# A two-layer recurrent and windowed-attention kernel: the second attention's key projection moves into free columns of the low-rank product

## The chip, the cores and the metric

The kernel runs on one core of one Trainium2 chip. The metric is the device time of one launch in microseconds (us), which covers all 16 sequences. In the text PE is TensorE, DVE is VectorE, ACT is ScalarE, POOL is GpSimd and SP is SyncE, whose queue issues every DMA transfer of this kernel.

## The reference, cut to what matters

Sixteen sequences of 1024 tokens with 256 features pass through two layers. Layer 0 is a gated recurrent attention with a mixture of experts as its gate. Layer 1, which the change touches, is attention in a window of 64 keys (16 query heads share 2 key/value heads of 16 features), gated by a two-matrix network with ternary weights and a low-rank term of rank 16.

```
def _L1_attn_ref(x, Wq, bq, Wk, bk, Wv, bv, Wo, bo):
    q = (x @ Wq + bq)...            # 16 heads of 16
    k = (x @ Wk + bk)...            # 2 heads of 16: 32 columns
    v = (x @ Wv + bv)...            # 2 heads of 16: 32 columns
    scores = jnp.einsum('bgrsd,bgswd->bgrsw', qg, k_win)   # window of 64 around each token
    probs = jax.nn.softmax(scores, axis=-1)
    ...
    return out @ Wo + bo

def _L1_ffn_ref(x, fast_b, w_fc, w_proj, u, v, gate):
    h = _bitlinear(x, w_fc) + gate * (x @ v.T @ fast_b.T @ u.T)
    r = jnp.maximum(h, 0.0)
    return _bitlinear(r * r, w_proj)

xn = _layernorm(x)
x = x + _L1_attn_ref(xn, ...) * _silu(_L1_ffn_ref(xn, ...))
```

## The kernel before, in words

One loop of two turns holds eight sequences written out one behind the other, so the body of a sequence runs 16 times. Each engine has its instructions in an order written out by hand; the engines meet only at semaphores. A sequence is cut into NC = 8 chunks of 128 tokens, and for wide products into NG = 2 groups of 512 tokens.

The stretch around the change is the seam between the layers. The layer-0 loop over the chunks `c` ends with `c = 7`. In it PE computes the recurrent outputs, turns (transposes) the normalised input of layer 1 into `xt`, two chunks at a time with `pair_turn`, and begins the projections of layer 1:

- `queries_keys(n)` for n = 0 to 5: three products of 512 columns for each group g = n // 3. Kinds 0 and 1 are the queries (`w_q2`, result `q2`, which lies in `qt`). Kind 2 is the keys: `w_k2r` holds the 32 key columns four times over, so the product puts the same 32 keys into all four groups of 32 rows. ACT evicts it twice (once for each key/value head, with `par_mask` as scale and `b_k2m` as bias, which zero the other head's rows) into `kt`, which lies in `k2`, shown as `k` in the rows.
- `low_rank(g)`: one product of 512 columns with `w_low`, whose 128 columns held the low-rank factor in columns 0, 32, 64 and 96 (16 each) and the two value heads in columns 16 to 31 and 48 to 63. ACT evicts it into `low_t`. Columns 80 to 95 and 112 to 127 were zero.
- `chunk_turn(6)` and `chunk_turn(7)`: the last two chunks of the layer-1 input are turned one at a time, since their normalisation comes late. ACT copies them out in `chunk_turned`.
- `output_turn(7)`, `output_turned(7)`, `output_project(7)`: the last output projection of layer 0 (PE, ACT into `yt`, PE).

After the seam comes the attention itself, a loop over the chunks: `score_masks(c)` puts the band mask into banks 1 to 4; `score_quad(c)` adds 32 small products of queries with keys, where group j of 32 rows works with `k2[32j:32j+32]`, so the keys must stand in all four row groups; DVE takes maxima and subtracts them (`maxima`, `shifted`); ACT takes the exponentials (`exps`); PE turns the probabilities (`probs_turn`, in two halves); ACT and DVE copy them out (`probs_turned`); PE multiplies by the values (`values`, `values_turn`). `window_values` turns the values out of `low_t`. `score_quad(3)` is the first that reads keys of the second group of 512 tokens.

The SP queue of one sequence holds the loads of `x`, the rows of the experts' gates, the loads of the next sequence's input behind the last `score_quad`, and the stores of the outputs. Before the loop SP also issues all weight and bias loads, one behind the other; PE's first product waits for all of them.

Of the kernel before, what the change touches and what calls it, by code (L numbers as in the profile page):

```python
# [48 lines left out]
def build_program(nc, a, out, n_seq):  # L49
# [107 lines left out]
    w_k2r = sb("w_k2r", [P, KD, 4, 2 * DH])  # L157
    w_o2 = sb("w_o2", [P, KD, D])
    b_q2 = sb("b_q2", [P, 2])
    b_k2 = sb("b_k2", [P, 1])  # L160
    b_k2m = sb("b_k2m", [P, 2])
# [58 lines left out]

    gate_dram = nc.dram_tensor("gate_rows", [NG, E, 512], F32, kind="Internal").ap()
# [41 lines left out]
    for g in range(2):  # L263
# [6 lines left out]
        for j in range(4):  # L270
            rows = slice(32 * j + 16 * g, 32 * j + 16 * g + 16)
            loads.append((b_q2[rows, :], bq_dram[g, j, :, :]))
            loads.append((b_k2[rows, :], a["L1_attn_bk"][g * DH:(g + 1) * DH].unsqueeze(1)))
        loads.append((b_low[32 * g + DH:32 * g + 2 * DH, :], a["L1_attn_bv"][g * DH:(g + 1) * DH].unsqueeze(1)))
    for k in range(KD):
# [9 lines left out]
             "st2 ve2 rs2 xn2_ok xt2p_ok xt2_ok qk2p_ok qk2_ok low_ok v2p_ok v2_ok sc_ok max_ok sub_ok "  # L285
# [7 lines left out]
    turn_banks = {6: 0, 7: 7}  # L293
# [3 lines left out]
    qk_banks = (2, 1, 4, 5, 6, 7)  # L297
    qk_done = (1, 2, 4, 5, 6, 8)
# [3 lines left out]
    for count, signals in (  # L302
# [3 lines left out]
            (4, "gkl_ok ve2 rs2 zexp_ok zln_ok xt_ok ft_ok zabs_ok gk_ok gkh_ok v2_ok z_ok v2p_ok "  # L306
             "xtp_ok zp_ok"),
            (5, "xt2_ok xt2p_ok"),
            (6, "qk_ok qkp_ok qk2p_ok"),
            (7, "end_ok ogam_ok ktok_ok gates_ok ssum_ok kp_ok ds_ok"),  # L310
            (8, "qx_ok hm_ok ove_ok ors_ok obet_ok hr_ok din_ok dout_ok dst_ok tg_ok tf_ok ots_ok "
             "yt_ok qk2_ok oc_ok o2t_ok tf2_ok gsel smid_ok vt_ok sg_ok f1_ok state_ok o1_ok "
             "onorm_ok y_ok f2_ok x_ok xn2_ok ptd_ok rden_ok o2_ok s2_ok nxn_ok f3_ok f4_ok y2_ok "
             "hp_ok cum_ok vg_ok f_ok ot_ok otok_ok ytp_ok s_ok pv_ok xp_ok o2tp_ok s2p_ok ftp_ok"),
# [4 lines left out]
            (64, "gl_ok"),  # L319
            (128, "xc_ok"),  # L320
# [154 lines left out]
    with nc.Block() as block:  # L475
# [61 lines left out]
        def _(dve):  # L537
# [30 lines left out]
            for r in (0, 2):  # L568
                link(nc.vector.tensor_copy(u_st[:, :, 32 * r:32 * r + RANK], u_hi[:].bitcast(F32)))
                link(nc.vector.tensor_copy(u_st[:, :, 32 * r + 32:32 * r + 32 + RANK], u_lo[:]))  # L570
# [14 lines left out]
            for k in range(KD):  # L585
                for r in range(4):
                    nc.vector.tensor_scalar(w_low[:, k, 32 * r:32 * r + RANK], bank[2 + k][:, 0:RANK],
                                            ffn_gate[:], None, ALU.mult)
# [122 lines left out]
    with nc.Fori(0, n_seq // UNROLL) as turn:  # L711
        with nc.Block() as block:

            @block.sync
            def _(sp):
                for copy in range(UNROLL):
# [7 lines left out]
                    for g in range(NG):  # L724
# [17 lines left out]
            def _(pool):  # L742
                for copy in range(UNROLL):
# [81 lines left out]
                    rstd2(3, NC - 1, NC)  # L825
                    for g in range(NG):
# [14 lines left out]
            def _(act):  # L841
                for copy in range(UNROLL):
# [85 lines left out]
                    def queries_keys(n):  # L928

                        g, kind = n // 3, n % 3  # L930
                        act.wait_ge(s["qk2p_ok"], at("qk2p_ok", n + 1))
                        cols = slice(g * 512, (g + 1) * 512)
                        if kind < 2:
                            nc.scalar.activation(q2[:, kind, cols], bank[qk_banks[n]][:], ACT.Identity,
                                                 bias=b_q2[:, kind:kind + 1]).then_inc(s["qk2_ok"], 1)
                        else:
                            for h in range(2):
# [4 lines left out]
                    for c in range(NC):  # L942
# [34 lines left out]
                        if c + 1 == NC:  # L977
                            experts_gate()
# [986 lines left out]
```

## Time and profile before

| | |
|---|---|
| median of 3 runs | 3582.03 us (3581.8 to 3582.57) |
| the profiled execution | 3582.19 us, its span 3580.5 us |
| PE busy | 3415.3 us, 95% |
| DVE, ACT, POOL busy | 72%, 53%, 35% |
| mean granted TensorE clock | 0.996 of full speed |

The profiled execution takes 1.7 us more than its span, for what lies around the first and the last instruction. A product in float32 stands in the trace as two records, so `low_rank`, with two products, is a row of x4. Matmuls are pipelined, their records overlap and their ends are modelled: what a step costs PE is read from the start of its row to the start of the next, and when its result is ready from the end of the row.

### The profile page before, as it was taken

How to read it: one execution, taken by the hardware profiler on the slowest of the kernel's cores; microseconds unless marked ns; L12 is line 12 of the kernel's file. 1: busy time of each engine (PE TensorE's matmuls, PEld its weight loads, DVE VectorE, ACT ScalarE, POOL GpSimd, SP SyncE). 2: the span in 40 equal slices, each digit the busy share in tenths (PEclk: the TensorE clock that was granted, in tenths of full speed). 3: DMA queues.
4: the chain of work that ended last, by engine and by line, in shares of the span. 5: the costliest groups of instructions: out<-in, count | busy, mean ns of one | idle time of the engine just before them, and what ended most of it. 6: DMA issues, size and time to landing. Idle time of an engine off the chain costs nothing. (4 is left out here: it accounts for less than half of the span.)

```text
span 3580.5 us, 89270 instructions
## 1 busy us (share of the span) xinstructions
PE 3415.3 (95%) x34684; PEld 2296.7 (64%) x34684; DVE 2586.4 (72%) x6184; ACT 1890.3 (53%) x4167; POOL 1255.6 (35%) x1457
## 2 busy tenths in 40 slices
PE   3999999999999999999989999999999999999998
PEld 2666666666666666666656666666666666666666
DVE  4677777777677776777767777777777767777677
ACT  1465463645636455464644646546365563646546
POOL 3524334232342424325233252433424234242432
PEclk9999999999999999999999999999999999999999
DMA  3101010010100101001010010101001010010100
GB/s 89 25 14 48 2 41 21 14 48 2 48 13 18 44 14 36 14 24 38 14 37 13 24 38 14 48 2 47 15 15 47 2 48 13 18 44 14 37 14 25
DMA packets 91023, 97.16 MB, mean 27 GB/s; under 512 B 19825, under 2 KB 73697, under 8 KB 90593
## 3 DMA queue, kind: packets, MB, share of 16 engines
q1 hardware_dynamic: 90592, 91.35, 9.6%
q8 instruction: 279, 4.57, 0.5%
q14 instruction: 152, 1.24, 0.1%
HBM read 74.01 MB, written 17.30 MB: 26 GB/s over the span
## 5 line engine op out<-in xcount | busy, mean ns | idle before, releaser
L834 POOL TENSOR_TENSOR qx<-qx 128x512 f32<-128x512 f32 x256 | 278.2, 1091 | 684.6 <-ACT qx L1081 683.7
L1344 DVE TENSOR_REDUCE row_max<-bank 128x4 f32<-128x384 f32 x512 | 271.9, 549 | 146.3 <-PE bank L1742 146.3
L1211 DVE TENSOR_TENSOR am<-bank,causal 128x512 f32<-128x512 f32 x512 | 328.2, 683 | 42.1 <-PE bank L1585 42.1
L1436 DVE TENSOR_TENSOR sq_lo<-qx,sq_hi 128x512 fp32r<-128x512 f32 x256 | 208.1, 813 | 193.1 <-ACT sq_hi L1060 192.6
L949 ACT ACTIVATE tanh_g<-bank 128x256 f32<-128x256 f32 x128 | 49.0, 383 | 405.7 <-PE bank L1474 405.7
L1474 PE MATMUL bank<-w_vg,xt 128*128 128x512 f32 x512 | 252.3, 615 | 0.0
L828 POOL TENSOR_TENSOR xl<-xt,xh 128x1024 fp32r<-128x1024 f32 x32 | 75.3, 2354 | 464.9 <-DVE xh L1406 464.9
L1515 PE MATMUL bank<-xt,w_down 128*128 128x512 f32 x512 | 237.2, 596 | 0.0
L1862 PE MATMUL bank<-sq_hi,pj_t 128*128 128x512 f32 x512 | 214.9, 420 | 16.4 <-DVE sq_lo L1436 9.9
L1353 DVE TENSOR_TENSOR am<-bank,row_max 128x384 f32<-128x384 f32 x384 | 212.8, 554 | 9.8
L999 ACT ACTIVATE am<-am 128x384 f32<-128x384 f32 x384 | 201.9, 526 | 9.9 <-DVE am L1353 3.3
L1081 ACT ACTIVATE qx<-bank,scale_fc 128x512 f32<-128x512 f32 x256 | 177.5, 693 | 56.0 <-PE bank L1849 56.0
L1862 PE MATMUL bank<-sq_lo,pj_t 128*128 128x512 f32 x512 | 202.0, 395 | 0.0
L747 POOL TENSOR_TENSOR qx<-qt,par_mask 128x512 f32<-128x512 f32 x128 | 136.2, 1064 | 177.9 <-ACT qt L447 138.3
L1060 ACT CAST sq_hi<-qx 128x512 fp32r<-128x512 f32 x256 | 158.9, 621 | 67.4 <-PE bank L1862 36.8
L1759 PE MATMUL bank<-ident,am 64*96 64x64 f32 x4096 | 167.0, 221 | 15.0 <-ACT qx L1015 14.7
L1759 PEld LDWEIGHTS bank<-ident,am 64*96 64x96 f32 x4096 | 131.0, 123 | 74.3 <-issue 55.3
L1270 DVE TENSOR_TENSOR state_sum<-bank,state_mid 128x256 f32<-128x256 f32 x112 | 47.4, 423 | 178.7 <-PE bank L1693 178.7
L1844 PE MATMUL bank<-xh,fc_t 128*128 128x512 f32 x512 | 171.3, 415 | 0.0
L756 POOL TENSOR_SCALAR o_veps<-o_mom 128x1 f32<-128x1 f32 x128 | 37.7, 295 | 370.2 <-DVE o_mom L1291 370.2
L1742 PE MATMUL bank<-k,qt 32*32 32x192 f32 x8192 | 164.0, 332 | 0.0
L1844 PE MATMUL bank<-xl,fc_t 128*128 128x512 f32 x512 | 160.2, 394 | 0.0
(263 smaller groups left out, 8827.0 us busy)
## 6 DMA issues: line engine op xcount, KB each, us to landing
g_wide<-gate_rows SPq DMA_DIRECT2D x64, 512.0 KB, 6.4
qt<-in_L_attn_x SPq DMA_DIRECT2D x136, 128.0 KB, 2.3
x<-in_L_attn_x SPq DMA_DIRECT2D x128, 128.0 KB, 2.2
out<-x SPq DMA_DIRECT2D x128, 128.0 KB, 1.7
x<-in_L_ffn_w_fc SPq DMA_DIRECT2D x1, 1024.0 KB, 5.8
attn<-in_L_ffn_w_proj SPq DMA_DIRECT2D x1, 1024.0 KB, 8.0
w_up<-in_L_ffn_Wu SPq DMA_DIRECT2D x1, 512.0 KB, 5.8
w_down<-in_L_ffn_Wd SPq DMA_DIRECT2D x2, 256.0 KB, 3.7
```

The lines of the kernel that those rows point to most:

```text
L834: nc.gpsimd.tensor_tensor(sq[:, n % 3, :], relu[:, n % 3, :], relu[:, n % 3, :], ALU.mult)\
L999: nc.scalar.activation(pr[:, j], pr[:, j], ACT.Exp).then_inc(s["pr_ok"], 1)
L1081: nc.scalar.activation(relu[:, n % 3, :], bank[1 + n % 3][:], ACT.Relu, scale=scale_fc[:, n % MT:n % MT + 1]).then_inc(s["relu_ok"], 1)
L1211: nc.vector.tensor_tensor(am_tiles[:, :, j], bank[3 + j][:].rearrange("p (f e t) -> p f e t", f=2, e=2), causal[:].unsqueeze(1).unsqueeze( ...
L1344: nc.vector.tensor_reduce(row_max[:, j, :], bank[1 + j][:, 0:4 * KW].rearrange("p (h k) -> p h k", k=KW), AX.X, ALU.max, negate=(j == 0)). ...
L1353: nc.vector.tensor_tensor(pr[:, j], bank[1 + j][:, 0:4 * KW].rearrange("p (h k) -> p h k", k=KW), row_max[:, j, :].unsqueeze(2).broadcast_ ...
L1436: nc.vector.tensor_tensor(sq_lo[:, n % 3, :], sq[:, n % 3, :], sq_hi[:, n % 3, :].bitcast(F32), ALU.subtract)\
L1474: mm = nc.tensor.matmul(dst, xt[:, k, c * P:(c + 1) * P], w[:, k, :], start=(k == 0), stop=(k == KD - 1))
L1515: mm = nc.tensor.matmul(bank[5 if g else j][:], w_down[:, k, j * P:(j + 1) * P], xt[:, k, g * 512:(g + 1) * 512], start=(k == 0), stop=(k ...
L1759: mm = nc.tensor.transpose(bank[5 + r][0:KW, h * QB:(h + 1) * QB], pr[rows, 2 * p + h // 4, h % 4, :], ident[rows, rows])
L1844: nc.tensor.matmul(h_bank, fc_t[:, k, m * P:(m + 1) * P], t[:, g, k, :], start=(t is xh and k == 0), stop=False)
L1862: mm = nc.tensor.matmul(bank[5 + o][:], pj_t[:, m, o * P:(o + 1) * P], part[:, n % 3, :], start=(m == 0 and part is sq_hi), stop=(m == MT ...
```

## The change

The keys' own product goes: `w_k2r`, its bias tiles and its two products of each sequence are removed. The 32 key columns now stand in columns 64 to 95 of `w_low`, and the low-rank factor in columns 0, 32, 96 and 112. `low_rank(g)` thus gives the keys once, in rows 64 to 95. Two masked copies (one for each head) put them into the same rows of `k2`: for the first group two ACT instructions (`key_halves`), for the second one POOL instruction. Then SP issues three transfers for each group, of 32 rows x 2 x 512 elements (128 KB) each, from rows 64 to 95 to the other three row groups. `score_quad(0)` and `score_quad(3)` wait for them (`kd_ok`).

The order at the seam changes too: `low_rank(0)` takes the place of `queries_keys(0)` in the last chunk of layer 0, `queries(0)` that of the key product, `score_masks(0)` and `score_quad(0)` stand ahead of `chunk_turn(7)`, and ACT copies `yt` ahead of the eviction of `queries(1)`. The loads ahead of the loop are 7 fewer (8 key biases go, one comes).

```diff
@@ loads ahead of the loop
             loads.append((b_q2[rows, :], bq_dram[g, j, :, :]))
-            loads.append((b_k2[rows, :], a["L1_attn_bk"][g * DH:(g + 1) * DH].unsqueeze(1)))
         loads.append((b_low[32 * g + DH:32 * g + 2 * DH, :], a["L1_attn_bv"][g * DH:(g + 1) * DH].unsqueeze(1)))
+    loads.append((b_low[key_rows, :], a["L1_attn_bk"].unsqueeze(1)))
...
+    rank_hi, rank_lo, key_rows = (0, 96), (32, 112), slice(64, 96)
...
-    turn_banks = {6: 0, 7: 7}
+    turn_banks = {6: 7, 7: 0}
-    qk_banks = (2, 1, 4, 5, 6, 7)
-    qk_done = (1, 2, 4, 5, 6, 8)
+    qk_banks = (5, 1, 6, 0)
+    low_banks = (2, 0)
@@ VectorE, ahead of the loop
+                nc.vector.tensor_copy(w_low[:, k, key_rows], w_kv2[:, k, 0, :])
-            for k in range(KD):
-                nc.vector.tensor_copy(w_k2r[:, k], w_kv2[:, k, 0, :].unsqueeze(1).broadcast_to([P, 4, 2 * DH]))
-            nc.vector.tensor_scalar(b_k2m[:], par_mask[:], b_k2[:], None, ALU.mult)
@@ SyncE, behind the gates' rows
+                    for g in range(NG):
+
+                        sp.wait_ge(s["kh_ok"], at("kh_ok", 2 + g))
+                        cols = slice(g * 512, (g + 1) * 512)
+                        for r in (0, 1, 3):
+                            sp.dma_start(kt[32 * r:32 * r + 32, :, cols], kt[key_rows, :, cols]).then_inc(s["kd_ok"], 16)
                     sp.wait_ge(s["sc_ok"], at("sc_ok", 4 * NC))
@@ GpSimd
                     rstd2(3, NC - 1, NC)
+
+                    pool.wait_ge(s["low_ok"], at("low_ok", 2))
+                    nc.gpsimd.tensor_tensor(kt[key_rows, :, 512:S],
+                                            low_t[key_rows, HALF + 512:HALF + S].unsqueeze(1).broadcast_to([2 * DH, 2, 512]),
+                                            par_mask[key_rows, :].unsqueeze(2).broadcast_to([2 * DH, 2, 512]), ALU.mult)\
+                      .then_inc(s["kh_ok"], 1)
+                    pool.wait_ge(s["kh_ok"], at("kh_ok", 3))
                     for g in range(NG):
@@ ScalarE
+                    def key_halves():
+
+                        act.wait_ge(s["low_ok"], at("low_ok", 1))
+                        for h in range(2):
+                            nc.scalar.activation(kt[key_rows, h, 0:512], low_t[key_rows, HALF:HALF + 512], ACT.Identity,
+                                                 scale=par_mask[key_rows, h:h + 1]).then_inc(s["kh_ok"], 1)
...
-                            queries_keys(0)
+                            low_rank(0)
...
                         if c + 1 == NC:
+                            key_halves()
                             experts_gate()
...
                     pair_turned(2)
-                    queries_keys(1)
                     output_turned(NC - 1)
-                    queries_keys(2)
+                    queries(1)
+                    queries(0)
                     chunk_turned(6)
-                    low_rank(0)
                     chunk_turned(NC - 1)
...
                     exps(0)
-                    queries_keys(3)
+                    queries(2)
                     exps(1)
-                    queries_keys(4)
+                    queries(3)
                     exps(2)
-                    queries_keys(5)
                     exps(3)
@@ TensorE
                     def score_quad(c):
 
+                        if c in (0, 3):
+                            pe.wait_ge(s["kd_ok"], at("kd_ok", 16 * 3 * (2 if c else 1)))
...
                     pair_turn(2)
-                    queries_keys(1)
+                    queries(1)
                     output_turn(NC - 1)
                     output_project(NC - 1)
-                    queries_keys(2)
+                    queries(0)
+                    chunk_turn(6)
+                    pe.wait_ge(s["low_ok"], at("low_ok", 1))
+                    pe.wait_ge(s["qk2_ok"], at("qk2_ok", 1))
+                    score_masks(0)
+                    pe.wait_ge(s["qk2_ok"], at("qk2_ok", 2))
+                    score_quad(0)
                     pe.wait_ge(s["sg_ok"], at("sg_ok", NC))
-                    chunk_turn(6)
-                    pe.wait_ge(s["f1_ok"], at("f1_ok", NC))
-                    low_rank(0)
                     chunk_turn(NC - 1)
-                    pe.wait_ge(s["qk2_ok"], at("qk2_ok", 4))
-                    score_masks(0)
-                    score_quad(0)
                     window_values(0)
-                    queries_keys(3)
-                    queries_keys(4)
-                    queries_keys(5)
-                    pe.wait_ge(s["qk2_ok"], at("qk2_ok", 6))
+                    queries(2)
+                    queries(3)
...
+                    pe.wait_ge(s["qk2_ok"], at("qk2_ok", 3))
                     probs_turn(0, 0)
```

In PE's order of one sequence the seam reads so before, from the last output projection of layer 0 (L1570) over the first key product (L1634 with `w_k2r`), `chunk_turn(6)`, `low_rank(0)` (L1719), `chunk_turn(7)`, masks, `score_quad(0)` (L1742) and `window_values(0)` (L1713) to the first turn of the probabilities (L1759):

```order
L1570 MATMUL bank<-w_out,yt 128x256 x2
L1634 MATMUL bank<-xt,w_k2r 128x512 x2
L1602 MATMUL bank<-ident,xn 128x128 x2
L1719 MATMUL bank<-xt,w_low 128x512 x2
L1602 MATMUL bank<-ident,xn 128x128 x2
L1731 MATMUL bank<-band_q,four_bf 128x384 x4
L1742 MATMUL bank<-k,qt 32x192 x32
L1713 MATMUL bank<-ident,low_t 96x64 x8
L1634 MATMUL bank<-xt,w_q 128x512 x4
L1634 MATMUL bank<-xt,w_k2r 128x512 x2
L1759 MATMUL bank<-ident,am 96x64 x16
```

And so now, from the same projection (L1582) to the same turn (L1772):

```order
L1582 MATMUL bank<-w_out,yt 128x256 x2
L1642 MATMUL bank<-xt,w_q 128x512 x2
L1614 MATMUL bank<-ident,xn 128x128 x2
L1742 MATMUL bank<-band_q,four_bf 128x384 x4
L1755 MATMUL bank<-k,qt 32x192 x32
L1614 MATMUL bank<-ident,xn 128x128 x2
L1730 MATMUL bank<-ident,low_t 96x64 x8
L1642 MATMUL bank<-xt,w_q 128x512 x4
L1772 MATMUL bank<-ident,am 96x64 x16
```

Both key products are gone, `low_rank(0)` has moved up into the last chunk, and the masks and `score_quad(0)` stand ahead of `chunk_turn(7)`.

ACT's order at the same place before, from the `yt` copy of chunk 6 (L907) to the exponentials of `exps(0)` (L1005):

```order
L907 COPY yt<-bank 128x256
L963 ACTIVATE tanh_f<-bank 128x256
L912 COPY xt<-bank 128x2x256
L934 ACTIVATE qt<-bank,b_q 128x512
L907 COPY yt<-bank 128x256
L938 ACTIVATE k<-bank,b_k2m,par_mask 128x512 x2
L917 COPY xt<-bank 128x2x128
L983 ACTIVATE low_t<-bank,b_low 128x512
L917 COPY xt<-bank 128x2x128
L1005 ACTIVATE am<-bank,row_max 128x96 x4
```

And now:

```order
L920 COPY yt<-bank 128x256
L958 ACTIVATE k<-low_t,par_mask 32x512 x2
L982 ACTIVATE tanh_f<-bank 128x256
L925 COPY xt<-bank 128x2x256
L920 COPY yt<-bank 128x256
L946 ACTIVATE qt<-bank,b_q 128x512 x2
L930 COPY xt<-bank 128x2x128 x2
L1018 ACTIVATE am<-bank,row_max 128x96 x4
```

The two key copies (L958) stand ahead of the last `tanh_f`; the second `yt` copy, of chunk 7, has passed the eviction of `queries(1)`.

SP's order now, from the second group of the experts' gates to the first load of the next sequence (L344); the rows `k<-k` are new, and what a row waits for stands in brackets:

```order
L726 DMA gate_rows<-low_t 8x512 [waits gx_ok]
L732 DMA g_wide<-gate_rows 64x4x512 [waits hm_ok,gw_ok]
L732 DMA g_wide<-gate_rows 64x4x512
L738 DMA k<-k 32x2x512 [waits kh_ok]
L738 DMA k<-k 32x2x512 x2
L738 DMA k<-k 32x2x512 [waits kh_ok]
L738 DMA k<-k 32x2x512 x2
L344 ISA [waits sc_ok]
```

The six new transfers stand between the gates, which are through by the middle of layer 0, and the wait for the last scores.

## Rows read from the trace of the kernel before

**Rows 1.** Page, part 1: busy us, share and instructions of each engine.

```profile
PE 3415.3 (95%) x34684; PEld 2296.7 (64%) x34684; DVE 2586.4 (72%) x6184; ACT 1890.3 (53%) x4167; POOL 1255.6 (35%) x1457
```

**Rows 2.** Waits of PE: who was waited for, total us, times, longest us.

```profile
PE bank L602 <- DMA w_down<-in_L_ffn_Wd: 46.6, 1, 46.6
...
PE bank L1570 <- ACT yt L907: 13.1, 16, 0.8
```

**Rows 3.** Timeline of PE at the seam: start us, us, line, tiles, [idle before].

```profile
187.75 1.96 PE L1634 MATMUL bank<-xt,w_q 128*128 128x512 f32 x4
189.54 0.38 PE L1557 MATMUL bank<-ident,y_tok 128*128 128x128 f32 x2
190.74 1.13 PE L1570 MATMUL bank<-w_out,yt 128*128 128x256 f32 x4 [0.82 <-ACT yt L907]
191.71 1.88 PE L1634 MATMUL bank<-xt,w_k2r 128*128 128x512 f32 x4
193.42 0.38 PE L1602 MATMUL bank<-ident,xn 128*128 128x128 f32 x2
193.64 1.88 PE L1719 MATMUL bank<-xt,w_low 128*128 128x512 f32 x4
...
195.67 0.34 PE L1731 MATMUL bank<-band_q,four_bf 32*128 32x384 bf16 x4
195.95 1.28 PE L1742 MATMUL bank<-k,qt 32*32 32x192 f32 x64
197.16 0.65 PE L1713 MATMUL bank<-ident,low_t 64*96 64x64 f32 x8
197.74 3.70 PE L1634 MATMUL bank<-xt,w_q 128*128 128x512 f32 x8
201.27 1.88 PE L1634 MATMUL bank<-xt,w_k2r 128*128 128x512 f32 x4
203.08 0.65 PE L1759 MATMUL bank<-ident,am 64*96 64x64 f32 x16
...
206.14 0.65 PE L1759 MATMUL bank<-ident,am 64*96 64x64 f32 x16 [0.92 <-ACT qx L1015]
...
218.31 1.28 PE L1742 MATMUL bank<-k,qt 32*32 32x192 f32 x64
```

**Rows 4.** Timeline of ACT at the seam.

```profile
184.35 0.37 ACT L907 COPY yt<-bank 128x256 f32<-128x256 f32 x1
187.28 0.38 ACT L963 ACTIVATE tanh_f<-bank 128x256 f32<-128x256 f32 x1 [2.56 <-PE bank L1616]
...
189.74 0.69 ACT L934 ACTIVATE qt<-bank,b_q 128x512 f32<-128x512 f32 x1 [1.44 <-PE bank L1634]
190.32 0.36 ACT L907 COPY yt<-bank 128x256 f32<-128x256 f32 x1
...
204.53 0.52 ACT L999 ACTIVATE am<-am 128x384 f32<-128x384 f32 x1
204.94 1.05 ACT L1015 COPY qx<-bank 96x512 f32<-96x512 f32 x2
...
208.75 0.69 ACT L983 ACTIVATE low_t<-bank,b_low 128x512 f32<-128x512 f32 x1
```

**Rows 5.** Timeline of DVE at the seam.

```profile
194.46 0.41 DVE L1204 TENSOR_SCALAR xn<-x,moments,rstd 128x256 f32<-128x256 f32 x1 [1.00 <-POOL rstd L785]
...
200.87 0.56 DVE L1353 TENSOR_TENSOR am<-bank,row_max 128x384 f32<-128x384 f32 x1
```

**Rows 6.** Groups of POOL's instructions: busy us, mean ns, idle before.

```profile
L828 POOL TENSOR_TENSOR xl<-xt,xh 128x1024 fp32r<-128x1024 f32 x32 | 75.3, 2354 | 464.9 <-DVE xh L1406 464.9
```

**Rows 7.** DMA issues: KB each, median us from issue to landing.

```profile
g_wide<-gate_rows SPq DMA_DIRECT2D x64, 512.0 KB, 6.4
qt<-in_L_attn_x SPq DMA_DIRECT2D x136, 128.0 KB, 2.3
```

**Rows 8.** Timeline of SP ahead of the loop.

```profile
43.16 4.25 SPq L342 DMA_DIRECT2D qt<-in_L_attn_x  x8
```

More of the change, by code:

```diff
@@ L567, in _ @@
             link(nc.vector.tensor_tensor(u_lo[:], u_nat[:], u_hi[:].bitcast(F32), ALU.subtract))
-            for r in (0, 2):
-                link(nc.vector.tensor_copy(u_st[:, :, 32 * r:32 * r + RANK], u_hi[:].bitcast(F32)))
-                link(nc.vector.tensor_copy(u_st[:, :, 32 * r + 32:32 * r + 32 + RANK], u_lo[:]))
+            for hi, lo in zip(rank_hi, rank_lo):
+                link(nc.vector.tensor_copy(u_st[:, :, hi:hi + RANK], u_hi[:].bitcast(F32)))
+                link(nc.vector.tensor_copy(u_st[:, :, lo:lo + RANK], u_lo[:]))
             dve.wait_ge(b_sem, 16 * 4)
@@ L585, in _ @@
             for k in range(KD):
-                for r in range(4):
-                    nc.vector.tensor_scalar(w_low[:, k, 32 * r:32 * r + RANK], bank[2 + k][:, 0:RANK],
+                for first_col in rank_hi + rank_lo:
+                    nc.vector.tensor_scalar(w_low[:, k, first_col:first_col + RANK], bank[2 + k][:, 0:RANK],
                                             ffn_gate[:], None, ALU.mult)
@@ L926, in _, with queries, low_rank @@
                     first_queries_keys(7)
-                    def queries_keys(n):
-                        g, kind = n // 3, n % 3
-                        act.wait_ge(s["qk2p_ok"], at("qk2p_ok", n + 1))
+                    def queries(n):
+                        g, kind = n // 2, n % 2
+                        act.wait_ge(s["qk2p_ok"], at("qk2p_ok", (2, 1, 3, 4)[n]))
                         cols = slice(g * 512, (g + 1) * 512)
[L933 to L937, printed above, removed]
-                                nc.scalar.activation(kt[:, h, cols], bank[qk_banks[n]][:], ACT.Identity,
-                                                     bias=b_k2m[:, h:h + 1], scale=par_mask[:, h:h + 1])\
-                                  .then_inc(s["qk2_ok"], 1)
+                        nc.scalar.activation(q2[:, kind, cols], bank[qk_banks[n]][:], ACT.Identity,
+                                             bias=b_q2[:, kind:kind + 1]).then_inc(s["qk2_ok"], 1)
+                    def low_rank(g):
+                        act.wait_ge(s["tp_ok"], at("tp_ok", g + 1))
+                        nc.scalar.activation(low_t[:, HALF + g * 512:HALF + (g + 1) * 512], bank[low_banks[g]][:],
+                                             ACT.Identity, bias=b_low[:]).then_inc(s["low_ok"], 1)
+                    def key_halves():
[3 more added lines that the diff above has]
+                                                 scale=par_mask[key_rows, h:h + 1]).then_inc(s["kh_ok"], 1)
                     for c in range(NC):
@@ L1665, in _ @@
                         else:
-                            queries_keys(0)
+                            low_rank(0)
                         if c == 0:
@@ L1715, in window_values @@
                         mm.then_inc(s["v2p_ok"], 1)
-                    def low_rank(g):
-                        for k in range(KD):
-                            mm = nc.tensor.matmul(bank[0 if g else 5][:], w_low[:, k, :],
-                                                  xt[:, k, g * 512:(g + 1) * 512], start=(k == 0), stop=(k == KD - 1))
-                        mm.then_inc(s["tp_ok"], 1)
                     def score_masks(c):
```

59 lines of the change are left out of this document (28 added, 31 removed).

## The prediction

> **What bounds the kernel now.** First the page's busy line: PE works 95% of the span, no other engine over 72% [rows 1]. So time taken out of PE's order comes back whole, unless a wait takes its place. Then PE's waits, for where it idles at the places touched: once in each of the 16 sequences it waits 0.8 us for `yt` at the last output projection of layer 0 [rows 2], and the timeline shows 0.92 us more ahead of the second half of the first turn of probabilities, at 206.14 [rows 3]. Last the timelines of PE, ACT and DVE through one seam, from 187.75 to 218.31, because only the order of releases there tells whether the freed time survives. That seam, one of 16 alike, is replayed below in the new order; the step from the start of a row to the start of the next is what PE pays, and its end is when ACT can begin.
>
> **Ahead of the loop.** PE's first product waits for all loads until 46.6 [rows 2], and they are issued one behind the other. Eight issues take 4.25 us, 0.53 each [rows 8]; 7 fewer are worth up to 3.7 us, and nothing if another transfer were the last to land. DVE loses two wide copies and one small one and gains two narrow ones. I take 3.5 us, nearer the full price, since PE's wait names the last load of the list as its releaser.
>
> **What goes from PE.** Two key products a sequence: 191.71 to 193.42 and 201.27 to 203.08, 1.71 and 1.81 us [rows 3], 3.52 us together. Those are the only products removed; `low_rank(0)` and `queries(0)` change places and have the same shape as the key product (1.88 us for each row of x4) [rows 3].
>
> **The `yt` copy.** Before, ACT evicted `queries(1)` at 189.74 and only then copied `yt`, 190.32 to 190.68 [rows 4], though PE's turn of `y_tok` ended at 189.92 [rows 3]. PE went on at 190.74. ACT begins about 0.03 us behind the end of a row: the product of 187.75 ends at 189.71 and its eviction starts at 189.74 [rows 3, 4]. Now the copy comes first: 189.95 to 190.31, PE at 190.37, a gain of 0.37 us. This edit stands in ACT's order alone.
>
> **Replay.** From there:
> - `output_project(7)` at 190.37 (0.97 us), `queries(0)` at 191.34 (1.71), `chunk_turn(6)` at 193.05 (0.22), masks at 193.27 (0.28), done at 193.55 (each step from [rows 3]).
> - `score_quad(0)` needs `queries(0)` evicted. Its products end 1.88 us behind their start, at 193.22; ACT evicts 193.25 to 193.94; PE starts at 193.99. A new wait of 0.44 us. Behind it in PE's order stand `chunk_turn(7)` and all the rest.
> - `score_quad(0)` takes 1.21 us, to 195.20. `chunk_turn(7)` needs the last normalised chunk, which DVE had ready at 194.87 [rows 5]; it does not wait. `window_values(0)` 195.42 to 196.00. ACT copies the turned chunk (a 0.36 us copy like that of `yt` [rows 4]) until about 195.97, so `queries(2)` starts at 196.02.
> - `queries(2)` and `queries(3)` take 3.53 us, to 199.55 [rows 3]. The first turn of probabilities needs `exps(1)`, which follows the eviction of `queries(2)` (products ready 197.90, evicted 198.6, exponential 199.1): no wait. That turn, masks and `score_quad(1)` take 0.6 + 0.28 + 1.21 us, to 201.6. The masks need DVE's last subtraction of chunk 0, at 201.43 before [rows 5]; `score_quad(0)` ends 1.96 us earlier, with a value copy now about 0.2 us later behind it, so 199.7, in time.
> - Then the second half of the turn waits for ACT: eviction of `queries(3)` from 199.74, two exponentials of 0.52 and two copies, 1.05 us together. Successive ACT rows overlap by 0.1 (204.53 + 0.52 against 204.94) [rows 4], so the copies start at 201.15 and end at 202.20; PE followed 0.15 us behind (205.99 to 206.14) [rows 3, 4]. PE goes on at 202.35.
>
> 206.14 - 202.35 = 3.79 us a sequence. As a check by pieces: 3.52 + 0.37 - 0.44 for the new wait + 0.2 for the old 0.92 that shrinks to about 0.7 = 3.65; the rest are small gaps in the old order. 16 x 3.79 = 60.6 us.
>
> **The copied keys, costed at nothing.** First group: `key_halves` is released when ACT has copied `yt` of chunk 6, at 184.72; two evictions of 512 elements at 0.69 make 186.1, and ACT's next instruction is due only at 187.28 [rows 4]. Without that gap they would push `tanh_f` back by 1.4 us. Three issues at 0.53 [rows 8] and a landing of 2.3 us, that of a 128 KB load [rows 7], give 189.5; with the 6.4 us of the 512 KB broadcasts [rows 7] it would be 193.6. PE asks at 193.99. Second group: `low_rank(1)` was evicted at 208.75 to 209.44 [rows 4], now 205.65. POOL's nearest row is the subtraction of as many elements per partition, 2.35 us [rows 6]; it ends at 208.05. The third issue starts at 209.1 and lands at 211.4. `score_quad(3)` was at 218.31 [rows 3], now 214.52: 3.1 us to spare. POOL's own next instruction waits for `xh`, which DVE makes only in chunk 1 of the attention, and SP's next wait is for the last scores; neither is delayed. A transfer from SBUF to SBUF over 32 partitions is not in this trace; between 2.3 and 6.4 us I take 2.3, since its bytes are those of that row. With 6.4 us it lands at 215.5, 1.0 us late.
>
> The trace shows 128 KB over 128 partitions landing in 2.3 us [rows 7]. The Trainium skill, page "SBUF — State Buffer", section "Door 1: The DMA port swizzle", states that 32 partitions reach only half of the 16 SBUF ports, about 218 GB/s, and that a transfer has some 2 us of fixed cost. By it three transfers of 128 KB, 0.39 MB, would need an estimated 3.8 us from the first issue. That would still end ahead of `score_quad(3)`, and the sum would be the same by the rule and by the row. No row of this trace shows a transfer between 32-partition ranges, so whether it holds here is open. It is the rule that speaks against the change, and it gives rival B its mechanism.
>
> **Sum.** 3582.2 (the profiled execution, 0.2 above the median of the runs shown) - 60.6 - 3.5 = 3518.1 us, 1.8% faster.
>
> **Rivals.**
> - A, the forecast: 3.4 to 4.1 us a sequence and 0 to 3.7 ahead of the loop, 3513 to 3528. Chance 0.74.
> - B, the copies of the second group come late: 1.0 us by the 6.4 us row, 16 us in all, 3534; if POOL's broadcast form is slower too, by 1 us more, 3550. For it: the form of transfer is unseen. Against it: 3.1 us of slack. Chance 0.08.
> - C, ACT and DVE, not PE, set the pace from `score_quad(0)` to the second turn of probabilities. Before, that took 197.16 to 206.14, 8.98 us [rows 3]. If the lag stays, PE goes on at 195.20 + 8.98 = 204.18, a gain of 1.96 a sequence: 3582.2 - 31.4 - 3.5 = 3547. Against it: part of the lag was the eviction of the second key product, which goes. Chance 0.10.
> - D, slower than before: the three copies clog each other, and `score_quad(3)` waits longer than everything gained, 3.79 + 0.2 us. That decides from a landing of 218.5 - 209.1 = 9.4 us per transfer on; at 12 us, say, 2.6 us a sequence are lost, 3624. The slowest landing in these rows is 6.4 us. Chance 0.02.
> - E, the change does nothing, because a chain without PE spans the seam, such as the last normalisation, through POOL and DVE (194.46 [rows 5]). PE now reaches `chunk_turn(7)` at 195.20 and finds it ready. 3582. Chance 0.02.
> - F, more is gained: the two waits at the seam, 0.44 and about 0.7 us, vanish as well, up to 16 x 1.1 us, 3500. Chance 0.04.
>
> **The numbers.** The time is that of A. The range takes A whole, B's first price and C: 3508 to 3547. A measurement of this kernel can tell about 0.2%, 7 us, from no change. Faster by more than that: A, B, C, F and the milder part of E, 0.96; within it 0.02; slower 0.02.
>
> **What the profile after would show.** PE's instructions fall by 128 records (two products of two records, twice a sequence, 16 times). The wait at the output projection shrinks from 0.8 to about 0.45 us. A new wait of about 0.4 us for the eviction of `queries(0)` stands ahead of `score_quad(0)`, released by ACT and not by a DMA. The step from that projection to the second half of the turn is 12.0 us instead of 15.4. The transfers `k<-k` land in 2 to 3 us, and no `score_quad(3)` waits. The first product starts near 43 us. A wait on `k<-k` would make B or D right; a longer wait at the second turn, C.

## The result, and the profile after

The changed kernel takes 3520.31 us (median of 4 runs, 3519.38 to 3520.95) against 3581.91 us before: a ratio of 0.983, with a 95% interval of 0.9812 to 0.9847. The prediction's sum was 3518.1. Its profiled execution took 3520.74 us with a span of 3519.0; before, the span was 3580.5. The granted clock was 0.996 in both.

The page's busy line of the changed kernel, to be held against [rows 1]:

```profile
PE 3365.3 (96%) x34556; PEld 2272.8 (65%) x34556; DVE 2584.2 (73%) x6183; ACT 1868.9 (53%) x4135; POOL 1286.4 (37%) x1473
```

PE lost 128 records and 50.0 us of busy time, but the span lost 61.5: the other 11.5 us were idle time of PE. POOL gained 16 instructions and 30.8 us, nearly all of it the copies of the second key group (16 x 1.89 = 30.2). Where PE's idle time is now, by its waits (total us, times, longest us), beside [rows 2]:

```profile
PE bank L602 <- DMA w_down<-in_L_ffn_Wd: 43.0, 1, 43.0
...
PE bank L1772 <- ACT qx L1028: 9.2, 16, 0.6
PE bank L1582 <- ACT yt L920: 7.4, 16, 0.5
...
PE bank L1755 <- ACT qt L946: 4.6, 16, 0.3
```

The first product starts 3.6 us earlier (43.0 for 46.6). The wait for `yt` is 7.4 us over the 16 sequences instead of 13.1. At `score_quad(0)` (L1755) stands a new wait, 0.3 us each time, and it is for ACT's eviction of the queries; no row names `k<-k` as a releaser. The same seam on PE's timeline, beside [rows 3] (start us, duration, line, tiles, idle before):

```profile
183.91 1.98 PE L1642 MATMUL bank<-xt,w_q 128*128 128x512 f32 x4
185.73 0.38 PE L1569 MATMUL bank<-ident,y_tok 128*128 128x128 f32 x2
186.58 1.13 PE L1582 MATMUL bank<-w_out,yt 128*128 128x256 f32 x4 [0.46 <-ACT yt L920]
187.54 1.88 PE L1642 MATMUL bank<-xt,w_q 128*128 128x512 f32 x4
189.26 0.38 PE L1614 MATMUL bank<-ident,xn 128*128 128x128 f32 x2
189.57 0.34 PE L1742 MATMUL bank<-band_q,four_bf 32*128 32x384 bf16 x4
190.20 1.28 PE L1755 MATMUL bank<-k,qt 32*32 32x192 f32 x64 [0.29 <-ACT qt L946]
191.41 0.44 PE L1614 MATMUL bank<-ident,xn 128*128 128x128 f32 x2
191.78 0.65 PE L1730 MATMUL bank<-ident,low_t 64*96 64x64 f32 x8
192.41 3.67 PE L1642 MATMUL bank<-xt,w_q 128*128 128x512 f32 x8
196.01 0.65 PE L1772 MATMUL bank<-ident,am 64*96 64x64 f32 x16
...
198.72 0.65 PE L1772 MATMUL bank<-ident,am 64*96 64x64 f32 x16 [0.58 <-ACT qx L1028]
199.31 1.98 PE L1652 MATMUL bank<-xt,w_low 128*128 128x512 f32 x4
...
210.90 1.28 PE L1755 MATMUL bank<-k,qt 32*32 32x192 f32 x64
```

From the row ahead of the last turn of `y_tok` to the second half of the turn of probabilities it is now 198.72 - 183.91 = 14.81 us; before, 206.14 - 187.75 = 18.39 us [rows 3]. That is 3.58 us gained per sequence. Over the whole loop it is the span's 61.5 less the 3.6 ahead of it, 57.9, divided by 16: 3.62. The two ways of reading agree within 0.04 us, but in part by luck, as the distance from one last output projection (L1570, now L1582) to the next shows. In most sequences it went from 217.06 to 213.49 us, 3.57 less. From the fourth to the fifth and from the twelfth to the thirteenth it fell by only 2.8 (to 214.2), where PE now waits 0.59 us for ACT in layer 0 (L1541), with the transfers and without. Over the turn of the loop it fell by 5.0 (230.76 to 225.78), because the granted clock stayed at half for 10.2 us there and for 13.7 before. Two sequences lost 1.5 us and the turn gained 1.4 beside the seam, and they cancel. Both lengths of the slow clock occur among the runs below, so two spans can differ by some 1.5 us for that alone.

ACT at this place, beside [rows 4]. The copies of the first key group (L958) come behind the `yt` copy of chunk 6, and `tanh_f` behind them still waits for PE, so they delay nothing. The second `yt` copy comes at once behind PE:

```profile
181.00 1.32 ACT L958 ACTIVATE k<-low_t,par_mask 32x512 f32<-32x512 f32 x2
183.54 0.38 ACT L982 ACTIVATE tanh_f<-bank 128x256 f32<-128x256 f32 x1 [1.22 <-PE bank L1628]
...
186.15 0.37 ACT L920 COPY yt<-bank 128x256 f32<-128x256 f32 x1 [1.59 <-PE bank L1569]
...
189.46 0.69 ACT L946 ACTIVATE qt<-bank,b_q 128x512 f32<-128x512 f32 x1 [2.22 <-PE bank L1642]
```

DVE's last normalised chunk, which `chunk_turn(7)` (191.41) needs, beside [rows 5]:

```profile
190.41 0.41 DVE L1216 TENSOR_SCALAR xn<-x,moments,rstd 128x256 f32<-128x256 f32 x1 [1.00 <-POOL rstd L791]
```

It ends at 190.82, 0.6 us early. The second key group goes through POOL and three transfers. First POOL's timeline, then SP's, then the page's row of the transfers (KB each, median us from issue to landing):

```profile
202.09 1.89 POOL L834 TENSOR_TENSOR k<-low_t,par_mask 32x1024 f32<-32x1024 f32 x1 [11.72 <-ACT low_t L951]
```

```profile
204.01 1.86 SPq L738 DMA_DIRECT2D k<-k  x3
```

```profile
k<-k SPq DMA_DIRECT2D x96, 128.0 KB, 2.4
```

The issues span 204.01 to 205.87; the third one's own starts at about 205.3, and with 2.4 us its copy has landed by 207.7. `score_quad(3)` asks at 210.90, so 3.2 us were to spare where 3.1 were forecast. That is the first sequence, and not all are alike. Over the 96 copies the view of the tile `k` says:

```profile
DMA to landing us min/median/max: 2.4/2.4/4.1
```

The slack at `score_quad(3)` lies between 1.5 and 3.25 us; it is least in the tenth sequence, where the third copy landed at 2143.97 and PE asked at 2145.47. At `score_quad(0)` it is 3.8 to 4.1 us.

### The profile page after: what moved, and what is told of

The parts are those of the page before. It is cut to its first block and busy times, and to the rows that moved or that the text cites. A ratio compares the mean times of both kernels' runs of the same rounds, so it can differ in the third digit from the quotient of the medians.

```text
span 3519.0 us, 89054 instructions
## 1 busy us (share of the span) xinstructions
PE 3365.3 (96%) x34556; PEld 2272.8 (65%) x34556; DVE 2584.2 (73%) x6183; ACT 1868.9 (53%) x4135; POOL 1286.4 (37%) x1473
## 5 line engine op out<-in xcount | busy, mean ns | idle before, releaser
L1772 PE MATMUL bank<-ident,am 64*96 64x64 f32 x4096 | 166.9, 221 | 9.7 <-ACT qx L1028 9.2
L1772 PEld LDWEIGHTS bank<-ident,am 64*96 64x96 f32 x4096 | 131.1, 123 | 69.4 <-issue 50.0
L1755 PE MATMUL bank<-k,qt 32*32 32x192 f32 x8192 | 164.0, 332 | 4.6 <-ACT qt L946 4.6
L1486 PEld LDWEIGHTS bank<-w_vg,xt 128*128 128x128 f32 x512 | 86.8, 189 | 98.4 <-issue 98.4
```

The costliest lines, as they stand in the source:

```text
L1486: mm = nc.tensor.matmul(dst, xt[:, k, c * P:(c + 1) * P], w[:, k, :], start=(k == 0), stop=(k == KD - 1))
L1755: mm = nc.tensor.matmul(bank[1 + j][b * WB:(b + 1) * WB, t * 2 * KW:(t + 1) * 2 * KW], q2[rows, t, first:first + WB], k2[rows, :, first:fi ...
L1772: mm = nc.tensor.transpose(bank[5 + r][0:KW, h * QB:(h + 1) * QB], pr[rows, 2 * p + h // 4, h % 4, :], ident[rows, rows])
```

## Experiments

**Seven loads put back.** After, with seven extra tiny loads (32 values each, into a tile that nothing reads) on the list ahead of the loop.

```diff
+    spare = sb("spare", [P, 8])
+    for i in range(7):
+        loads.append((spare[key_rows, i:i + 1], a["L1_attn_bk"].unsqueeze(1)))
```

> The changed kernel with seven more loads of 32 values each, into a spare tile, put behind the load of the key bias, so that as many loads are issued ahead of the loop as before the change. Nothing else differs. If the issues set the start of PE's first product (the forecast), that product moves from 43.0 us back to about 46.5 and the launch is 3.2 to 3.7 us longer than the changed kernel, about 3524. If the last load's landing or DVE's own preparation sets it, the launch stays at 3520.

Measured: 3524.5 us (3523.32 to 3524.93), ratio to before 0.9837 (0.9824 to 0.9851), against 3520.31 for after. PE's first wait, which was 43.0:

```profile
PE bank L605 <- DMA w_down<-in_L_ffn_Wd: 46.5, 1, 46.5
```

It is 3.5 us longer and the median 4.2. On SP's timeline the seven stand right ahead of the load of `w_down`, whose issue moves from 38.47 to 41.99:

```profile
38.45 3.50 SPq L617 DMA_DIRECT2D spare<-in_L_attn_bk  x7
```

The loads' bytes are next to nothing; it is the number of issues ahead of the last weight that PE pays for, here 0.50 us each.

**The `yt` copy alone.** Before, with ACT's copy of the last `y_tok` turn ahead of its eviction of `queries(1)` and of the key product.

```diff
-                    queries_keys(1)
                     output_turned(NC - 1)
+                    queries_keys(1)
                     queries_keys(2)
```

> The kernel before with one edit: ACT copies yt of the last chunk ahead of the eviction of the second query product. If PE's time comes back whole, the wait of 0.82 us shrinks to about 0.46 and 16 x 0.36 = 5.8 us go: about 3576. The rival, that the earlier output projection only lengthens the wait at the last turned chunk or at the second half of the first turn of probabilities, gives 3581 to 3582.

Measured: 3575.75 us (3574.42 to 3577.18), ratio 0.9981 (0.9972 to 0.999), some 6.3 us faster than before. Its waits:

```profile
PE bank L1570 <- ACT yt L907: 7.4, 16, 0.5
...
PE bank L1759 <- ACT qx L1015: 14.7, 16, 0.9
```

The wait went from 13.1 to the same 7.4 us that the changed kernel has, 5.7 us, and the wait at the second half of the turn of probabilities stayed. Another 0.6 us of the 6.3 lie ahead of the loop (first wait 46.0 for 46.6), where the edit changes nothing. The step stands alone, as the prediction said.

**The products put back in time.** After, with each low-rank product computed twice over (the second pass repeats both contraction halves), so that PE has its two products a sequence again, and everything else stays.

```diff
-                        for k in range(KD):
+                        for k in (0, 1, 0, 1):
```

> The changed kernel with each low-rank product computed twice into the same bank (the first result is overwritten), so PE has as many products as before the change, while the order, the copies of the keys and the ACT work stay as changed. If the removed products are what brought the gain and nothing hides them, 16 x 2 x 1.72 = 55 us come back: about 3575. If part of the second product falls into a wait for ACT or DVE, less: each wait at the seam is at most 0.6 us, so not under 3556. If the gain came from the new order and not from the products, it stays near 3520.

Measured: 3570.85 us (3569.45 to 3572.68), ratio 0.9969 (0.9957 to 0.9981): 50.5 us more than after, 3.16 a sequence. PE's timeline at the second low-rank product, which was 1.98 us for x4 at 199.31:

```profile
198.38 0.66 PE L1772 MATMUL bank<-ident,am 64*96 64x64 f32 x16 [0.58 <-ACT qx L1028]
198.97 3.70 PE L1652 MATMUL bank<-xt,w_low 128*128 128x512 f32 x8
202.60 1.08 PE L1790 MATMUL bank<-qx,v 96*32 96x128 f32 x32
```

The doubled one takes 202.60 - 198.97 = 3.63 us where it took 201.22 - 199.31 = 1.91: 1.72 more, and the same for the other makes 3.44 a sequence. On the clock it is 3.16 by the medians and 48.7 / 16 = 3.04 by the spans. PE's waits did not take up the rest: they sum to 128.3 us in both traces, and the one for ACT is 0.58 in both. The page's busy line of this kernel shows where it went:

```profile
PE 3414.0 (96%) x34684; PEld 2296.8 (64%) x34684; DVE 2585.3 (72%) x6183; ACT 1867.2 (52%) x4135; POOL 1286.7 (36%) x1473
```

PE's busy time rose by the same 48.7 us as the span. So other rows got shorter: 0.2 us of it is found at one place, ahead of the last turn of `y_tok`, where the turn of a pair of chunks (L1607) takes 0.43 us to the next row (183.21 to 183.64) for 0.57 (183.34 to 183.91), and `queries(1)` 1.75 (to 185.39) for 1.82 (to 185.73). Another 0.08 stands right behind the first low-rank product, where the four products with `state_mid` take 0.54 to the next row (178.45 to 178.99) for 0.62 (178.50 to 179.12). What a product added to PE's time here is thus its own step less about a tenth, without any wait. All the same this is the main term, shown from the other side.

**Transfers off.** After, without the six transfers; the two waits on them are waits on the key copies of the one row group instead. The scores of the other three row groups are thus made from stale keys.

```diff
-                        for r in (0, 1, 3):
-                            sp.dma_start(kt[32 * r:32 * r + 32, :, cols], kt[key_rows, :, cols]).then_inc(s["kd_ok"], 16)
...
-                            pe.wait_ge(s["kd_ok"], at("kd_ok", 16 * 3 * (2 if c else 1)))
+                            pe.wait_ge(s["kh_ok"], at("kh_ok", 3 if c else 2))
```

> The changed kernel without the six transfers of each sequence and with the two waits for them replaced by waits for the masked copies in rows 64 to 95. The scores of the other three row groups are computed from stale keys; the instructions of all compute engines are unchanged. If the transfers are hidden (the forecast: 3.1 us of slack), the time is that of the changed kernel, 3520, within 2 us. If they cost something by disturbing other transfers or the engines' reads, it is faster by more than 3 us.

Measured: 3520.87 us (3520.61 to 3521.74), ratio 0.9828 (0.9815 to 0.9842), span 3519.0, the same as after to the tenth. Where they stand, the transfers cost nothing that can be measured, neither as a wait nor by contention.

**Transfers one behind the other.** After, where each of the three copies of the second group waits for the landing of the last.

```diff
-                        for r in (0, 1, 3):
+                        for i, r in enumerate((0, 1, 3)):
                             sp.dma_start(...)
+                            if g:
+                                sp.wait_ge(s["kd_ok"], at("kd_ok", 16 * (3 * g + i + 1)))
```

> The changed kernel, but SP issues each transfer of the second group only when the one before has landed, and waits for the last one too. In the changed kernel's trace the three issues start at 204.0 to 205.3, each lands 2.4 us behind its issue, 207.7 at the latest, and score_quad(3) starts at 210.9. One behind the other they land near 206.5, 209.0 and 211.5. If landing is all that counts, score_quad(3) waits 0.6 to 0.9 us for the copies in each sequence and the launch is 10 to 14 us longer than the changed kernel, about 3532. If the slack is larger than the trace shows, it stays at 3521; if transfers to row groups one at a time are slower, 3540 or more.

Measured: 3539.59 us (3538.44 to 3540.3), ratio 0.9879 (0.9864 to 0.9894), 19.3 us above after. PE waits now for the transfers:

```profile
PE bank L1757 <- DMA k<-k: 12.2, 16, 2.2
```

The waits sum to 12.2 us, yet the kernel lost 19.3, and more than the forecast of 10 to 14. The waits are uneven: 0.2 to 0.8 us in most sequences, but 2.08, 2.20 and 2.23 in the fourth, the eighth and the last. In each of these three one copy took 3.53, 3.70 or 3.65 us from issue to landing, where the median is 2.4. Two rows of the timeline, of the first and the fourth sequence:

```profile
211.32 1.28 PE L1757 MATMUL bank<-k,qt 32*32 32x192 f32 x64 [0.37 <-DMA k<-k]
...
855.08 1.61 PE L1757 MATMUL bank<-k,qt 32*32 32x192 f32 x64 [2.08 <-DMA k<-k]
```

Behind the long wait the same row takes 1.61 us. The windows around it (stretch: length, PE busy, PEld, DVE, ACT, POOL, PEclk, DMA share, GB/s):

```profile
852.70:855.10 2.40, 0.32 (x8) 0.08 (x7) 1.23 (x3) 0.71 (x2) 1.03 (x1) 1.00 0.26 55
855.10:859.10 4.00, 4.00 (x85) 2.69 (x86) 1.72 (x4) 1.10 (x4) 1.32 (x1) 0.57 0.00 0
859.10:862.00 2.90, 2.78 (x56) 1.94 (x54) 2.83 (x6) 2.42 (x8) 0.00 (x0) 1.00 0.02 6
```

For some 4 us behind the wait the granted clock is 0.57 on the mean, then 1.00 again. From the output projection of this sequence to the next it took 217.67 us for 214.22 in after, 3.45 more, of which 2.08 is the wait. The eighth sequence lost 3.63 us in the same way, and the last 4.90 (121.10 us from its output projection to the end for 116.20), where the granted clock was 0.59 on the mean over 7.6 us behind the wait. So a late copy is dearer than its wait: by the spans the kernel lost 18.9 us, of which 12.2 are waits, 5.5 lie behind the three long waits beside a slow clock, and 1.2 are not assigned.

**Copies twice.** The same, with the three copies of the second group made twice over, six in series, and PE waiting for all.

```diff
-                        for r in (0, 1, 3):
+                        for i, r in enumerate((0, 1, 3, 0, 1, 3) if g else (0, 1, 3)):
                             sp.dma_start(...)
+                            if g:
+                                sp.wait_ge(s["kd_ok"], at("kd_ok", 16 * (3 * g + i + 1)))
...
-                            pe.wait_ge(s["kd_ok"], at("kd_ok", 16 * 3 * (2 if c else 1)))
+                            pe.wait_ge(s["kd_ok"], at("kd_ok", 16 * 3 * (3 if c else 1)))
```

> The changed kernel, but the three transfers of the second group are made twice, all six one behind the other, and score_quad(3) waits for the sixth. With 2.5 us each from 204.0 on they land near 219, so it waits about 8 us a sequence. If only the wait counts, 16 x 8.1 = 130 us come on top of 3520: 3650. In the run with three transfers one behind the other the granted clock fell to half for some 3.5 us behind the waits of 2.1 us and more; if that follows here in every sequence, 1.3 to 1.8 us more each, about 3675. Either way slower than the kernel before (3582), which is the point from which the rival on the other side would have been right.

Measured: 3682.32 us (3676.46 to 3682.69), ratio 1.0279 (1.0263 to 1.0294), slower than before. The wait, its first instance, and the windows behind that instance:

```profile
PE bank L1757 <- DMA k<-k: 127.3, 16, 9.8
```

```profile
217.72 1.95 PE L1757 MATMUL bank<-k,qt 32*32 32x192 f32 x64 [7.38 <-DMA k<-k]
```

```profile
219.00:221.00 2.00, 2.00 (x49) 1.08 (x19) 1.02 (x2) 0.37 (x1) 0.00 (x0) 0.50 0.04 8
...
223.00:225.00 2.00, 1.90 (x49) 1.32 (x48) 1.91 (x4) 0.86 (x3) 0.00 (x0) 0.93 0.00 0
```

The profiled run is the fastest of the four, 3676.46 us, against forecasts of 3650 (the wait alone) and 3675 (with the clock). Its span is 155.7 us longer than after's: 127.3 of waits and 28.4 left over, 1.8 us a sequence, beside a clock at 0.50 (1.2 GHz) in place of 1.00 (2.4 GHz) behind each wait. The 0.93 in the stretch from 223 to 225 puts the return at 223.3, 5.6 us behind the wait's end; the fall came before that end (0.51 from 213.0 to 217.7, with PE idle). This is rival D made real: a wait of 8.0 us a sequence and its clock cost more than the 3.62 that the change gained.

**The turn of chunk 7 ahead of the scores.** After, with `chunk_turn(7)` back in its old place ahead of the masks and `score_quad(0)`.

```diff
                     queries(0)
+                    pe.wait_ge(s["sg_ok"], at("sg_ok", NC))
+                    chunk_turn(NC - 1)
...
-                    pe.wait_ge(s["sg_ok"], at("sg_ok", NC))
-                    chunk_turn(NC - 1)
```

> The changed kernel with the turn of the last chunk back ahead of the masks and of the first score_quad, as in the kernel before. In the changed kernel PE ends the turn of chunk 6 at 189.57 and DVE has the last normalised chunk at 190.82, so PE would wait about 1.2 us there, start score_quad(0) near 191.4 instead of 190.2 and queries(2) near 193.2 instead of 192.4. If that replay holds: 0.8 us a sequence, about 13 us, 3533. If the order is only a matter of taste because a later wait takes it up, 3520 to 3523.

Measured: 3537.53 us (3536.89 to 3538.44), ratio 0.9873 (0.9858 to 0.9888), 17.2 us above after. Waits and timeline of PE:

```profile
PE bank L1614 <- DVE xn L1216: 21.4, 16, 1.3
```

```profile
190.97 0.41 PE L1614 MATMUL bank<-ident,xn 128*128 128x128 f32 x2 [1.33 <-DVE xn L1216]
```

PE now waits 1.33 us a sequence for the last normalised chunk, and the 0.29 us for the queries is hidden behind it: 21.4 - 4.6 = 16.8 of the 17.2 us. The forecast of 13 was too low: `queries(2)` starts at 193.38 where 193.2 was put, so 1.0 us is lost and not 0.8. In the new kernel the order of the two steps is worth 1.05 us of the 3.62. The granted clock stayed 1.00 behind this wait (stretch 191 to 195).

**Scores' halves exchanged.** After, where `score_quad(0)` takes its second half of heads first and waits for the eviction of `queries(0)` only ahead of the other half.

```diff
-                        for t in range(2):
+                        for t in ((0, 1) if c else (1, 0)):
+                            if c == 0 and t == 0:
+                                pe.wait_ge(s["qk2_ok"], at("qk2_ok", 2))
...
-                    pe.wait_ge(s["qk2_ok"], at("qk2_ok", 2))
                     score_quad(0)
```

> The changed kernel with the two halves of score_quad(0) in the other order: the 16 products that need only queries(1) first, then the 16 that need queries(0), whose eviction PE waits for only then. If PE alone sets the pace, the wait of 0.29 us goes in each sequence: 4.6 us, about 3516. If ACT sets it from there on (the exponentials and copies ahead of the second half of the first turn of probabilities), the gain only lengthens the wait of 0.58 us there and the time stays at 3520.

Measured: 3516.23 us (3515.03 to 3516.97), ratio 0.9814 (0.98 to 0.9827), 4.1 us below after. The row that had a wait of 0.29:

```profile
189.69 1.28 PE L1757 MATMUL bank<-k,qt 32*32 32x192 f32 x64
```

The wait for ACT at the second half of the turn of probabilities stayed at 0.58 us each time, so it didn't take up the gain: PE, and not ACT, sets the pace here.

**The last low-rank product split.** After, with `low_rank(1)`'s first contraction half ahead of the second half of the turn of probabilities, as work for PE during the wait of 0.58 us.

```diff
+                            low_rank(1, (0,))
                         probs_turn(c, 1)
...
-                            low_rank(1)
+                            low_rank(1, (1,))
```

> The changed kernel with the two products of low_rank(1) divided: the first stands ahead of the second half of the first turn of probabilities, where PE now waits 0.58 us for ACT, the second stays behind it. If the wait is filled and the second product still covers the copies that the first values product needs, 0.58 us a sequence go: 9 us, about 3511. If the values product then waits for those copies instead, little or nothing: 3517 to 3521.

Measured: 3517.26 us (3517.11 to 3520.5), ratio 0.9819 (0.9806 to 0.9833). The median is 3.1 us below after, its slowest run lies among those of after. Only a third of the expected gain is there, and the waits say why:

```profile
PE bank L1804 <- ACT o_turned L1036: 6.3, 16, 0.4
```

The old wait is gone, and a new one of 0.4 us stands four rows later. ACT's order is unchanged, but where it idled 0.35 us ahead of the copy of the turned values (202.37 in after), it now still has to evict the low-rank product (200.92, 0.70 us), and makes the copy at 201.49; PE waits for it until 202.14. Of 0.58 us a sequence 0.18 is left, 2.9 us in all.

**Both.** The last two edits together.

> The changed kernel with both edits: the halves of score_quad(0) exchanged (alone 3516.2) and low_rank(1) divided (alone 3517.3). If the two waits are independent the gains add, 4.4 + 3.3 = 7.7 us: 3513. If ACT sets the pace behind the seam, only the larger remains: 3516.

Measured: 3513.44 us (3512.19 to 3515.95), ratio 0.9808 (0.9794 to 0.9821), span 3510.8. The gains add: 4.1 + 3.1 = 7.2, measured 6.9. It is the fastest of these kernels, faster than before and than the change as made.

## Why the prediction was right

The mechanism and the sum held: 3518.1 forecast, 3520.31 measured, 2.2 us apart, rival A. The sum starts from the profiled execution before; the one after took 3520.74, 2.6 us more than the sum.

- **PE is the bound and its time comes back.** Shown from both sides: two products less a sequence and the waits that they held up gave 3.62 us (3.57 in most sequences), and two products put back took 3.0 to 3.2. Of the 3.52 us put for the two products PE's busy time shows 50.0 / 16 = 3.13: the rows that stay got longer by the rest. The waits gave back 0.36 (`yt`) and 0.34 (14.7 - 9.2 over 16 sequences) and took 0.29.
- **Ahead of the loop, 3.5 us.** Measured 3.6 in the trace; seven tiny loads put back cost 3.5 in the wait. The full price of an issue was the right end of the bounds, and at 0.50 to 0.51 us it was a little under the 0.53 that was put.
- **The `yt` copy, 0.37 us.** The wait shrank by 0.36 (0.82 to 0.46), and by the same sum where the edit stood alone. From row to row it is 0.32: 190.74 - 187.75 = 2.99 before, 186.58 - 183.91 = 2.67 after. ACT starts 0.04 us behind the end of the turn (186.11, 186.15) where 0.03 was put.
- **The new wait at `score_quad(0)`.** Forecast 0.44, measured 0.29, for the releaser named. The row started 3.62 us behind the output projection (190.20 - 186.58), exactly as forecast (193.99 - 190.37): the eviction's end was right. PE was busy 0.15 us longer ahead of it. `chunk_turn(6)` took 0.31 for 0.22; and the masks were put at 0.28, their step with a row behind them, where PE that goes idle behind them is counted to the end of the row, 0.34.
- **Behind the score quad** the steps were charged too low: `chunk_turn(7)` 0.37 for 0.22, `window_values` 0.63 for 0.58, `queries(2)` and `queries(3)` 3.60 for 3.53; the first turn of probabilities stood 9.43 us behind the projection instead of 9.18. The piece that ACT ends made up for some of it: 2.71 us from that turn to its second half (198.72 - 196.01) where 2.80 were forecast. The wait there was 0.58 us for "about 0.7". So the stretch from the projection came to 12.14 us for 11.98. With 0.05 us at the `yt` copy this is the gap between 3.79 and 3.58, and 60.6 - 57.9 = 2.7 us, less 0.1 ahead of the loop, is the whole error of the sum; that the 57.9 fit the seam so well is in part the luck of the two parts outside it that cancel. The mis-sized term is mainly the step of short rows: 0.22 for a `chunk_turn` was read at one place, and in the new ones it is 0.31 and 0.37. The trace of before had a second one, ahead of the masks as `chunk_turn(6)` is now, and its step to the masks at 195.67 is the same 0.31:

```profile
195.36 0.38 PE L1602 MATMUL bank<-ident,xn 128*128 128x128 f32 x2
```

- **Keys at nothing.** Measured: without the transfers the span is the same 3519.0. Between 2.3 and 6.4 us the row of like bytes was the one to take: 2.4. POOL's broadcast product took 1.89 us, less than the 2.35 of its nearest row; the issues took 0.62 each where 0.53 was put; both errors together left the slack at 3.2 for 3.1 in the first sequence. The landing was taken as one number, and it is not: in the tenth sequence the slack was 1.5 us. The three transfers took 207.7 - 204.0 = 3.7 us from the first issue in the first sequence, and 2143.97 - 2138.57 = 5.4 in the tenth. The estimate from the Trainium skill, page "SBUF — State Buffer", was 3.8 us, with the rate from section "Door 1: The DMA port swizzle" and the fixed cost from section "The DMA setup-cost knee"; the trace agrees with it in the first sequence and not in the tenth, and it can't show whether ports or issues set the 3.7.
- **Rival B** would have needed a landing 3.2 us later in the first sequence and 1.5 us later in the tenth, so it was nearer than its row of 6.4 us made it look; even copies in series, which reach PE in 0.2 to 0.8 us of wait in most sequences, cost only 19.3 us. **C** fell: the stretch from the end of `score_quad(0)` to the second half of the turn shrank from 8.98 to 7.31 us (198.72 - 191.41), by nearly the key product's step, and the run with the halves exchanged shows that time gained ahead of it comes through. **D** is real where forced (3682.32 us), and its price per us of wait is higher than forecast, since the clock drops as well. **E** fell: `chunk_turn(7)` did not wait, but in its old place it would have (1.33 us), so 17 of the 58 us in the loop need the new order and not only the removal. **F** is partly to be had: 6.9 us of the two waits, by two more edits.

## What to carry to other kernels

On the bound engine, price a removed instruction at its full step, then replay the seam row by row in the new order with the other engines' durations: here this found the one new wait at the seam and its releaser, and was off by 0.2 us in 3.79; the 0.59 us of wait in two sequences of layer 0 it could not find, since one seam was replayed for all sixteen. Take the step of a short row from a place with the same row behind it. A copy that leaves the bound engine is free only while it is early, so work out its slack with the longest landing and not only the median, and fill a wait only after looking at what the engine that released it does next.

## What the runs showed that was not expected

- A wait of PE costs more than itself once it is long. Behind waits of 0.3 to 1.33 us the granted clock stayed 1.00; behind the wait of 2.08 us it was 0.57 on the mean for 4 us, behind another of 2.23 us 0.59 for 7.6 us, and behind 7.38 us it was 0.50, back at 1.00 some 5.6 us after the wait's end. The extra cost worked out as 1.4 us (3.45 - 2.08), 2.7 us (4.90 - 2.23), and 1.8 us (28.4 / 16) a sequence. PE was idle ahead of each of these drops.
- The copies between row groups of SBUF, 128 KB over 32 partitions, landed in 2.4 us at the median, 0.1 us behind a load of the same size over 128 partitions (2.3 us, [rows 7]).
- The copies that landed late all had a load of instructions beside them. The traces of after, copies in series and copies twice hold 336 copies between row groups. In 211 of them no transfer of kind `instruction` (the page's part 3) was in flight between issue and landing, and all landed in 2.35 to 2.48 us. In the other 125 one was; 22 of these took over 3 us, up to 4.42, among them the three late ones behind the waits of over 2 us. Whether the one causes the other was not tried.
- Products put into PE's order added 3.04 us a sequence to its busy time, not the 3.44 of their own steps, and products taken out gave 3.13, not 3.52: rows near the seam changed their steps. What couples them stays open.
